# Gated delta rule on one core: decay exponents from BF16 pieces of running gate sums, two ScalarE jobs moved in, one copy placed earlier

## The reference

```python
mixed = silu(causal_conv4(x @ w_qkv, conv_w))
q, k, v = split(mixed)
beta = sigmoid(x @ w_b)
g = -(exp(A_log) * softplus(x @ w_a + dt_bias))
q = l2norm(q) * DK ** -0.5; k = l2norm(k)
def step(state, q_t, k_t, v_t, g_t, b_t):
    state = state * exp(g_t)
    delta = (v_t - k_t @ state) * b_t
    state = state + outer(k_t, delta)
    return state, q_t @ state
core = norm_w * rmsnorm(core) * silu(x @ w_z)
out = core @ w_out
```

## Time and profile before

| what | value |
|---|---|
| time, median of 3 runs | 3851.72 us (3851.08 to 3855.5) |
| the profiled execution | 3852.4 us, of which the span of the trace is 3850.5 us |
| granted TensorE clock, mean over the span | 0.964 |
| busy time of TensorE, VectorE, ScalarE, GpSimd | 3585.6, 2884.1, 2310.9, 1948.8 us |
| decay products L1546, 256 instructions | 134.0 us busy |
| masks `gu` L1846, 512 instructions | 156.6 us busy |
| `scale_v` L2072, 128 instructions | 82.0 us busy |
| copies of the unit matrix L1928, 64 instructions | 25.4 us busy |

### The profile page before, as it was taken

The page is one execution under the profiler, slowest core; times in us unless marked ns, Lnnn a source line. Parts: engine busy times, 40 slices in busy tenths (PEclk is TensorE's granted clock), DMA queues, the critical chain, the costliest instruction groups (busy, mean ns, idle before and its releaser), DMA issues. The chain is left out here.

```text
span 3850.5 us, 69510 instructions
## 1 busy us (share of the span) xinstructions
PE 3585.6 (93%) x22926; PEld 2257.6 (59%) x22926; DVE 2884.1 (75%) x6989; ACT 2310.9 (60%) x6075; POOL 1948.8 (51%) x4645
## 2 busy tenths in 40 slices
PE   7999999998897689999999999999999999999789
PEld 3233323324554467777777777777777777777545
DVE  6888888883325478888888888888888888888633
ACT  2266666675133566677677677667667667666420
POOL 2000000001304387777777777777777777777310
PEclk9699999998798799999999999999999999999989
DMA  3100000000632011111111111111111111111100
GB/s 112 54 18 17 17 18 18 9 1 8 238 94 85 16 23 40 30 34 39 30 39 34 30 40 33 30 40 33 30 41 32 30 41 33 29 41 24 44 6 17
DMA packets 271636, 148.70 MB, mean 39 GB/s; under 512 B 222385, under 2 KB 251058, under 8 KB 270002
## 3 DMA queue, kind: packets, MB, share of 16 engines
q1 hardware_dynamic: 268210, 135.88, 13.2%
q0 software_dynamic: 3072, 8.39, 0.7%
HBM read 102.30 MB, written 41.68 MB: 37 GB/s over the span
## 5 line engine op out<-in xcount | busy, mean ns | idle before, releaser
L1916 POOL TENSOR_TENSOR dl_blocks_tmp<-dl_blocks_l,dl_blocks_x 128x60 f32<-128x60 f32 (+24 forms) x1984 | 734.6, 370 | 334.4 <-DMA dl_blocks_l<-lm_dram 193.7
L1921 POOL TENSOR_TENSOR dl_blocks_x<-dl_blocks_x,dl_blocks_tmp 128x60 f32<-128x60 f32 (+24 forms) x1984 | 707.3, 357 | 155.5
L540 DVE TENSOR_REDUCE part_max<-mx 128x1 f32<-128x512 f32 x1024 | 637.0, 683 | 83.3 <-PE mx L396 83.2
L472 ACT ACTIVATE normed_t<-sc 128x1024 f32<-128x1024 f32 x512 | 496.3, 1021 | 224.2 <-PE sc L409 223.9
L2103 DVE SCALAR_TENSOR_TENSOR dl_conv<-dl_raw,dl_weights,dl_conv 128x512 f32<-128x512 f32 x768 | 574.7, 776 | 14.6 <-ACT dl_conv L1813 3.9
L1583 PE MATMUL prep<-normed_t,dl_weights 128*128 128x512 f32 x1024 | 485.2, 597 | 5.3 <-ACT dl_conv L1813 4.3
L1762 ACT ACTIVATE dl_q_state<-rec_a,t_neg_decay 128x128 f32<-128x128 f32 x512 | 160.0, 364 | 399.3 <-DVE dl_r L2003 399.3
L396 PE MATMUL mx<-k_t,q_t 96*128 96x512 bf16 x1024 | 375.7, 402 | 16.0 <-DVE part_max L540 8.8
L377 POOL TENSOR_TENSOR v_staged<-v,v_bias 128x256 f32<-128x256 f32 x16 | 11.5, 721 | 694.8 <-PE o_ps L421 694.7
L1688 PE MATMUL gate_y_ps<-dl_w_out,dl_gated_t 128*128 128x256 f32 x1024 | 282.6, 398 | 77.4 <-ACT dl_gated_t L1768 77.4
L409 PE MATMUL sc<-q_t,k_t 99*128 99x512 bf16 x1024 | 306.0, 381 | 0.6
(11 more groups left out here) (290 smaller groups left out, 7730.6 us busy)
## 6 DMA issues: line engine op xcount, KB each, us to landing
dl_blocks_l<-lm_dram SPq DMA_DIRECT2D x256, 128.0 KB, 2.6
dl_weights<-in_w_delta SPq DMA_DIRECT2D x16, 776.0 KB, 4.4
lm_dram<-dl_lm SPq DMA_DIRECT2D x256, 32.0 KB, 1.7
xs_dram<-dl_blocks_x SPq DMA_DIRECT2D x256, 32.0 KB, 2.0
dl_inverse_t<-xs_dram SPq DMA_DIRECT2D x256, 32.0 KB, 1.8
qk_dram<-k_t SPq DMA_DIRECT2D x16, 384.0 KB, 2.6
k_t<-qk_dram SPq DMA_DIRECT2D x96, 64.0 KB, 2.2
q_t<-qk_dram SPq DMA_DIRECT2D x96, 64.0 KB, 2.2
```

The lines of the kernel that those rows point to most:

```text
L472: act.activation(probs[:, e % 2, u * 2 * BQ:(u + 1) * 2 * BQ], flat(sc[u][:, :, :]), ACT.Exp, scale=float(DH) ** -0.5).then_inc(s["exp_don ...
L540: dve.reduce_max(part_max[:, t % NT, x[2]:x[2] + 1], bank_of(x)[:, :], AX.X).then_inc(s["ring_read"], 1)
L1916: pool.tensor_tensor(out, L[:, 0:i, i].unsqueeze(1).broadcast_to([P, NM - c0, i]), Xs[:, c0:NM, i:i + 1].broadcast_to([P, NM - c0, i]), AL ...
L1921: pool.tensor_tensor(Xs[:, c0:NM, 0:i], Xs[:, c0:NM, 0:i], out, ALU.add).then_inc(s["solve_step"], 1)
```

## The change

- The gate sums are made in period 0: `gate_sums` (TensorE) moves from the start of period 1 to slot 10 of period 0. Their running sums are copied over g (`gate_sum_copy`), turned by four transposes (`turn_gate_sums`), split on VectorE into three BF16 pieces (`split_sums`) and stored to DRAM.
- For each quad SP loads the pieces twice, as rows that are multiplied by ones and as columns of a pattern of ones and minus ones (`gate_rows_in`). `decays` is then one BF16 product of 27 rows per half quad. `gates` goes. GpSimd makes the pattern once, among the masks.
- `scale_v` moves from VectorE to ScalarE, slot 8, as four instructions of 256 columns in place of two of 512.
- The copy of the unit matrix moves from GpSimd to ScalarE, slot 6 (`unit_block`).
- The last of the four `copy_gated` moves from slot 14 to slot 13, behind `copy_blocks` and ahead of `silu`.
- The set-up uses one semaphore where it had two.

```diff
-                pe.matmul(flat(bank[:, :, :]), tab["after"], flat(gu[:, GM * g:GM * g + GM, :]), start=True, stop=False)
+                pe.matmul(flat(bank[:, :, :]), gate_cols[:, :], flat(gate_rows[:, GM * g:GM * g + GM, :]), start=True,
+                          stop=False)
...
+            def gate_rows_in(n):
+                kh, q = head_of(n)
+                if n:
+                    sp.wait_ge(s["d_mm"], 2 * n)
+                src = a["gate_pieces"][NT * VH * kh + NM * q:NT * VH * kh + NM * (q + 1), :, :]
+                sp.dma_start(gate_rows[0:PIECES, :, :], src.rearrange("m s i -> s m i")).then_inc(s["rows_in"], 16)
+                sp.dma_start(gate_cols[PIECES:GATE_ROWS, :], src.rearrange("m s i -> (m s) i")).then_inc(s["rows_in"], 16)
...
             for n in PERIODS:
                 front, prep, merge, late = quads_of(n)
+                if front is not None:
+                    gate_rows_in(front)
...
+            def turn_gate_sums():
+                pe.wait_ge(s["act_link"], 5)
+                for b in range(NT * HV // P):
+                    last = pe.transpose(IB[0][:, b * P:(b + 1) * P], flat(tab["g"])[:, b * P:(b + 1) * P], c.ident[:, :])
+                last.then_inc(s["ab_done"], 1)
...
+            def scale_v(p, i):
+                act.wait_ge(s["tv_mm"], 2 * p + i + 1)
+                act.wait_ge(s["norm_done"], p + 1)
+                for j in range(2):
+                    out = vr_[p % 3][:, 2 * i + j, :, :].rearrange("p h d -> p (h d)")
+                    last = act.activation(out, IB[i][:, 2 * j * P:2 * (j + 1) * P], ACT.Copy,
+                                          scale=norm_k[:, 2 * i + j:2 * i + j + 1])
+                last.then_inc(s["vr_done"], 1)
...
-            def gates(n):
...
+            def unit_block(p):
+                if p >= 2:
+                    act.wait_ge(s["x_out"], 64 * (p - 1))
                 else:
+                    act.wait_ge(s["masks_done"], MASK_STEPS + UNIT_STEPS)
+                act.activation(flat(Xs_[p % 2][:, :, :]), flat(tab["unit"]), ACT.Copy).then_inc(s["unit_in"], 1)
...
-                    if slot in (2, 5, 9, 14) and is_chunk(g - 2):
+                    if slot in (2, 5, 9) and is_chunk(g - 2):
                         copy_gated(g - 2)
...
+                        if slot == 6:
+                            unit_block(prep)
+                        if slot == 8:
+                            scale_v(prep, 0)
+                            scale_v(prep, 1)
                     if merge is not None and slot == 13:
                         copy_blocks(merge)
+                    if slot == 13 and is_chunk(g - 2):
+                        copy_gated(g - 2)
                     if front is not None:
                         if slot == 4:
                             halo(front)
-                            gates(front)
...
             def start_blocks(p):
-                if p >= 2:
-                    pool.wait_ge(s["x_out"], 64 * (p - 1))
-                pool.tensor_copy(Xs_[p % 2][:, :, :], tab["unit"]).then_inc(s["solve_step"], 1)
-                steps[0] += 1
-                pool.wait_ge(s["solve_step"], steps[0])
+                pool.wait_ge(s["unit_in"], p + 1)
...
+            def split_sums():
+                turned = IB[0][:, :].rearrange("p (b i) -> p b i", i=P)
+                dve.wait_ge(s["ab_done"], 2)
+                linked(dve.tensor_copy(pieces[:, :, 0, :], turned), 7)
+                linked(dve.tensor_tensor(rest, turned, pieces[:, :, 0, :], ALU.subtract), 8)
+                linked(dve.tensor_copy(pieces[:, :, 1, :], rest), 9)
+                linked(dve.tensor_tensor(pieces[:, :, 2, :], rest, pieces[:, :, 1, :], ALU.subtract), 10)
...
-                        if slot == 8:
-                            scale_v(prep, 0)
-                            scale_v(prep, 1)
```

More of the change, by code:

```diff
@@ L1323 @@
 ROOT_ROW = 22
-SOLVE_STEPS = 2 + 2 * (BLK - 1)
-MASK_STEPS = 7
-GATE_STEPS = 12
+SOLVE_STEPS = 1 + 2 * (BLK - 1)
+PIECES = 3
+GATE_ROWS = PIECES + PIECES * NM
+MASK_STEPS = 11
+UNIT_STEPS = 7
+GATE_STEPS = 16
 AFTER_L = 2
@@ L1374, in delta_heads @@
         tmp = f("blocks_tmp", [P, NM, BLK])
-        gu = f("g_upto", [P, NM, P])
+        gate_rows = f("gate_rows", [GATE_ROWS, NM, P], BF16)
+        gate_cols = f("gate_cols", [GATE_ROWS, P], BF16)
         junk = f("junk", [P, 12, DK], BF16)
@@ L1395, in delta_heads @@
             "p (t n) -> p t n", t=NT) for i in range(2))
+        rest = flat(attn_[DEPTH - 1][:, :, :])[:, 0:NT * HV].rearrange("p (b i) -> p b i", i=P)
+        pieces = flat(attn_[DEPTH - 2][:, :, :]).bitcast(BF16)[:, 0:PIECES * NT * HV].rearrange(
+            "p (b s i) -> p b s i", s=PIECES, i=P)
         ab_in = c.sem(ctx, "dn_ab_in")
@@ L1537, in decays @@
             def decays(n, p, g):
[L1538 removed]
+                pe.wait_ge(s["rows_in"], 32 * (p + 1))
                 if g == 0 and n >= 3:
@@ L1737, in _ @@
                             turn_v(n, prep, 1)
+                    if n == 0 and slot == 10:
+                        gate_sums()
+                    if n == 0 and slot == 12:
+                        turn_gate_sums()
                     if front is not None and slot in (5, 7, 9, 11):
@@ L1835, in scale_out @@
                 act.activation(w_out(kh), w_out(kh), ACT.Copy, scale=tab["norm_w"]).then_inc(s["w_scaled"], 1)
-            def gates(n):
-                kh, q = head_of(n)
-                if n:
-                    act.wait_ge(s["d_mm"], 2 * n)
-                else:
-                    act.wait_ge(s["gate_link"], 6)
-                    act.wait_ge(s["masks_done"], MASK_STEPS)
-                for ch in range(QC):
-                    for h in range(VH):
-                        last = act.activation(gu[:, VH * ch + h, :], tab["upto"], ACT.Copy,
-                                              scale=tab["g"][:, QC * q + ch, VH * kh + h:VH * kh + h + 1])
-                last.then_inc(s["gu_done"], 1)
+            def unit_block(p):
+                if p >= 2:
+                    act.wait_ge(s["x_out"], 64 * (p - 1))
+                else:
+                    act.wait_ge(s["masks_done"], MASK_STEPS + UNIT_STEPS)
+                act.activation(flat(Xs_[p % 2][:, :, :]), flat(tab["unit"]), ACT.Copy).then_inc(s["unit_in"], 1)
             def act_linked(ins, n):
@@ L1863, in decay_tables, with gate_sum_copy @@
             def decay_tables():
+                for i, name in enumerate(("neg_decay", "decay_after", "chunk_decay")):
+                    act_linked(act.activation(flat(tab[name]), sums[i], ACT.Exp), 6 + i)
+            def gate_sum_copy():
                 act.wait_ge(s["summed"], 1)
-                for i, name in enumerate(("neg_decay", "decay_after", "chunk_decay")):
-                    act_linked(act.activation(flat(tab[name]), sums[i], ACT.Exp), 5 + i)
+                by_head = flat(tab["g"]).rearrange("p (k t h) -> p k t h", t=NT, h=VH)
+                act_linked(act.activation(by_head, sums[0].rearrange("p (t k h) -> p k t h", t=NT, h=VH), ACT.Copy), 5)
             gate_logs()
@@ L1899, in _ @@
                             projected(front, (5, 7, 9, 12).index(slot))
+                        if n == 0 and slot == 9:
+                            gate_sum_copy()
+                        if n == 0 and slot == 12:
+                            decay_tables()
                         if slot == 13:
@@ L1962, in masks @@
                 sel(tab["neg"], [[-1, P]], 0, 1, ALU.is_gt)
+                linked(pool.memset(gate_cols[:, :], 1.0))
+                linked(pool.memset(gate_rows[:, :, :], -1.0))
+                sel(gate_rows[:, :, :], [[-PIECES, NM], [0, P]], -PIECES, 1, ALU.is_ge)
+                sel(gate_rows[:, :, :], [[PIECES, NM], [0, P]], 2 * PIECES - 1, -1, ALU.is_ge)
                 linked(pool.memset(tab["half"], 0.5))
@@ L2213, in _ @@
                             convolve(front, m, k)
+                    if n == 0 and slot == 13:
+                        split_sums()
                     if merge is not None and slot == 15:
@@ L2312 @@
         aps[name] = nc.dram_tensor(f"in_{name}", arr.shape, mybir.dt.from_np(arr.dtype), kind="ExternalInput").ap()
+    aps["gate_pieces"] = nc.dram_tensor("gate_pieces", (NT * HV, PIECES, P), BF16).ap()
     aps["lm_dram"] = nc.dram_tensor("lm_dram", (NM, BLOCKS, BLK, BLK), F32).ap()
```

46 lines of the change are left out of this document (19 added, 27 removed).

## The result

The changed kernel takes **3798.3 us** (median of 4 runs, 3783.16 to 3802.59) against 3853.21 us (4 runs, 3851.08 to 3855.5): ratio **0.985**, 95% interval 0.9821 to 0.988, faster by far more than the 0.2% that can be told apart. The forecast was 3790 us in a range of 3740 to 3830. The profiled execution took 3802.59 us, 3800.7 of it span.

A forecast was written before the change was run, and what follows sets the result against it. TensorE was taken to bound the kernel at 35.86 us a period, the ring to bind next; 35.19 - 0.43 + 0.1 = 34.86 us, so 60 x 1.00 + 2.5 = 62.5 us off 3852.4 gave 3790 us, range 3740 to 3830.

The forecast's parts named there:

- The ring: VectorE block matrices, store and load, GpSimd's twenty solve rows and a root, VectorE gate: no period under 35.19 us.
- Either half of TensorE's saving: Copy ahead (1.27 us wait) or decay products (1.32 us a period): with the wait kept TensorE needs 34.54, under 34.86.
- Relief of 0.43 us: GpSimd's solve in each period: one of twelve VectorE convolutions no longer meets it, 0.43 us less, bounds 0 and 0.86.
- Late stores, 0.1 us: SP's block-matrix stores: one period in seven takes 2.49 us instead of 1.78, adding 0.1 us to the period.
- the start: Period 0 and the first decay product: 2.5 us of gain, between 0 and 4.
- the rival without relief: Convolutions still meet GpSimd's solve twelve times: period 35.19 us, time 3810 us; chance 0.15.
- The terms of TensorE: Per period: copy wait 1.27 us gone, two decay products at 0.21 us save 1.32; TensorE alone needs 33.27 us.
- TensorE stays the bound: Rival: VectorE's part after the root can move, so the period is 33.27 us, time 3694 us; chance 0.12.
- Nothing for masks, unit matrix, SP: ScalarE's masks removed, unit matrix moved off GpSimd, two more SP loads a quad: each worth nothing in the steady state.
- The slower rival: Convolutions close up on rows 31 to 20 of GpSimd's solve, 0.43 us each; with three more 3887 us; chance 0.05.

The follow-up runs named there:

- copy_back_roots: Changed kernel with the fourth copy_gated back in slot 14 and two GpSimd roots issued earlier in the solve: 3785.29 us, ratio 0.9831, period 34.85 us.
- copy_only: Kernel before with one edit, the last copy_gated in slot 13 ahead of the table load: 3814.64 us, ratio 0.9909, period 35.33 us.
- scale_back: Changed kernel with scale_v back on VectorE, two instructions in slot 8 ahead of the convolution: 3806.47 us, ratio 0.9894, period 35.29 us.

## Why the prediction was right, and where it was off

- **TensorE bound the kernel before.** Right, and shown: two roots moved out of the way change nothing there, and the copy moved as well takes its period from 35.86 to 34.74 us.
- **The ring is next, at 35.19 us.** Right. With the copy alone, periods without a late store last 35.21 us; with one root issued five rows earlier 37 us fall off.
- **Either half of TensorE's saving is enough.** Right: without the copy's move the time is 3798.45 us (TensorE would then need 34.85 us by copy_back_roots, where I had 34.54: still under the ring), and the decays add 0.04 us a period to the copy (copy_only beside scale_back).
- **Relief of 0.43 us: mis-sized.** "With the 1.28 us of `scale_v` out of VectorE's list the first convolution ends before the load lands, so one meeting of twelve goes." The first half came true: it ends at 2177.99 + 0.74 = 2178.73, and the load lands at 2179.53. But the second and third, which were to wait for other engines, moved up with it and now fall on the first two instructions of the solve. They start at 2179.32, 0.21 us ahead of its first instruction; before, they started 2202.60 - 2201.45 = 1.15 us behind it. VectorE has no idle time ahead of them in either kernel:

```profile
2202.60 1.40 DVE L2103 SCALAR_TENSOR_TENSOR dl_conv<-dl_raw,dl_weights,dl_conv 128x512 f32<-128x512 f32 x2
```

In the mean of 56 periods the solve's first two instructions went from 0.54 and 0.29 us to 0.59 and 0.54, the fourth and fifth from 0.56 and 0.52 to 0.25 and 0.26. GpSimd's part of the ring is 28.14 us where it was 28.26: 0.12 of relief. What I had missed is that this stretch of the list moves as a whole; the meeting that went was replaced by the next one.
- **Late stores, 0.1 us: too much.** In the changed kernel 12 of 57 periods (quads 6 to 62) have a load that goes out over 3.3 us after the block matrices' end instead of 3.11, by 0.68 us more in the mean, and the period that follows is 35.12 us against 35.05 for the others: 0.01 us over all periods. In scale_back, 11 such periods, late by 0.62, are followed by 35.62 against 35.19. So the move of `scale_v` pays in a way that I hadn't listed: a solve that begins late finds the pair of convolutions over, and so gains on its first rows what it lost. That and the relief, 0.14 us in undisturbed periods, make the 0.22 us of scale_back.
- **Sum.** The forecast had 60 x 1.00 + 2.5 = 62.5 us, the trace gives 47.2 us of the steady stretch. For the start it gives 1.1 us from quad 0's block matrices to quad 3's (97.16 us before, 96.03 now); before quad 0 it can't be read: quad 0's block matrices end between 1293.8 and 1305.1 us in the profiles of runs whose code is the same up to there (scale_back and copy_back_roots are the ends). The medians differ by 54.9 us, with an interval of 46 to 69 from the ratio. The measured 3798.3 us lie 8 us over the forecast and 12 under the rival without relief (3810): the time alone would not have told the two apart, and the period of 35.07 us lies nearer to that rival's 35.19 than to 34.86.
- **The terms of TensorE, which didn't decide:** the new product takes 0.30 to 0.31 us, not 0.21. The 0.21 was read off the BF16 product of slot 1; the same product in slot 2 of the kernel before takes 2222.17 - 2221.86 = 0.31 us, a row nearer to what the new product then took:

```profile
2221.86 0.38 PE L1547 MATMUL prep<-t_neg,identb 128*128 128x512 bf16 x1
2222.17 1.14 PE L1635 MATMUL merge_ps<-dl_inverse_t,dl_lm 64*64 64x64 f32 x16
```

The copy and the decays together are worth 35.86 - 33.88 = 1.98 us, not 2.59. Had the rival "TensorE stays the bound" held, its 3694 us would have been too low by some 32 us; with the roots moved it is 3725.55.
- **Nothing for masks, unit matrix, SP.** No engine shows a wait on the two new loads or the unit matrix, and SP's store of the block matrices still waits for VectorE (470.7 us in 56 periods). These parts were not undone one by one.
- **The slower rival.** The convolutions did close up on the solve, as it says, but one for one. The ground given against it, that all but the first wait for other engines, did not hold for the second and third.

## What to carry to other kernels

Before costing a saving on the busiest engine, follow the ring of other engines that returns to the same instruction one iteration later, and add it up without the waits: its length is the floor, and here it left 0.79 us a period of the 1.98 that TensorE was spared. Then look on that ring for an instruction that only stands late in its list: two roots of 0.7 us, moved ahead of five and of four rows of the solve, gave the changed kernel 73 us, more than either half of the change, though they gave the kernel before nothing. An edit that only shifts a list against its neighbour's doesn't remove a contention by itself; it changes which instruction meets which.
